# Moving one layer norm's last step, one gating product and one bias add within the order of work of a fused transformer kernel's last stage

## What is computed

```python
y = y_shared + w0 * expert0(x) + w1 * expert1(x)     # two experts' sums
x = x + layernorm(y)
out = (linear_attention(layernorm(x)) @ Wo) * sigmoid(x @ G1 @ G2)   # gated attention output
x = x + (layernorm(out) * gamma + beta, normed once more)
# 4th block: two time steps (a pair of tiles), t = 0, 1
c = f * c + i * g
h = tanh(x @ wo.T + c_final @ uo.T + bo)             # "the state's output" is c_final @ uo.T + bo
x = x + layernorm(h)                                 # a pair's last norm, then its store
```

## Time and profile before

| what | value |
|---|---|
| time, median of 3 runs | 1462.52 us (1462.14 to 1462.62) |
| the profiled execution | 1463.27 us |
| its span, first to last instruction | 1461.4 us |
| granted TensorE clock, mean | 0.988 of full speed |
| busy, whole span: PE / PEld | 1410.7 us (97%) / 1235.5 us (85%) |
| busy, whole span: DVE / ACT / POOL | 871.8 us (60%) / 715.1 us (49%) / 603.8 us (41%) |

### The profile page before, as it was taken

One profiled execution on the slowest core, in us unless ns is written; L12 is line 12 of the kernel. 1 busy time (PEld: TensorE's weight loads), 2 busy tenths in 40 slices (PEclk: granted clock), 3 DMA queues, 4 the chain that ended last, 5 costly groups with the idle time before them and its releaser, 6 DMA issues. The chain is left out here.

```text
span 1461.4 us, 36312 instructions
## 1 busy us (share of the span) xinstructions
PE 1410.7 (97%) x13257; PEld 1235.5 (85%) x13257; DVE 871.8 (60%) x1979; ACT 715.1 (49%) x1656; POOL 603.8 (41%) x1133
## 2 busy tenths in 40 slices
PE   7999999899999999999999999999999999999985
PEld 6888888788999999999999999876777778777875
DVE  5888888365333344334433332466888888888772
ACT  4666666222454444444444543343555555555542
POOL 3655665124221222122112210735667776775442
PEclk9999999899999999999999999999999999999997
DMA  6434334253111111111111111531111221121000
GB/s 188 125 110 125 115 109 121 80 156 118 37 38 44 44 41 41 52 44 41 41 44 49 44 41 51 179 98 44 56 49 49 63 60 52 46 62 38 9 16 22
DMA packets 88733, 100.11 MB, mean 68 GB/s; under 512 B 12432, under 2 KB 75664, under 8 KB 88560
## 3 DMA queue, kind: packets, MB, share of 16 engines
q1 hardware_dynamic: 80704, 78.51, 17.4%
q0 software_dynamic: 6480, 17.70, 4.3%
q10 hardware_dynamic: 1376, 1.57, 0.3%
HBM read 63.28 MB, written 34.47 MB: 67 GB/s over the span
## 5 line engine op out<-in xcount | busy, mean ns | idle before, releaser
L1073 DVE TENSOR_TENSOR ex_gT<-ex_gT,wa_xk 128x256 f32<-128x256 f32 x71 | 29.9, 422 | 306.2 <-ACT ex_gT L1036 306.2
L938 POOL COPY slot_idx<-source 128x1 int32<-128x1 int32 x69 | 37.6, 545 | 403.1 <-PE wa_Z L995 388.2
L968 PE MATMUL wa_P<-ex_xT,lane_w 128*128 128x128 f32 x1704 | 202.0, 275 | 0.0
L968 PEld LDWEIGHTS wa_P<-ex_xT,lane_w 128*128 128x128 f32 x1704 | 196.1, 192 | 0.2 <-issue 0.2
L1004 PE MATMUL wa_Y<-w,ex_gT 128*128 x852 | 195.8, 380 | 0.4 <-issue 0.4
L1004 PEld LDWEIGHTS wa_Y<-w,ex_gT 128*128 128x128 f32 x852 | 156.4, 190 | 18.9 <-issue 0.7
L968 PE MATMUL wa_qv<-ex_xT,lane_w 128*128 128x128 f32 x852 | 118.2, 275 | 0.0
L968 PEld LDWEIGHTS wa_qv<-ex_xT,lane_w 128*128 128x128 f32 x852 | 111.9, 192 | 3.6
L964 ACT COPY lane_w<-w 128x1408 f32 x71 | 96.9, 1365 | 7.8 <-issue 1.6
L1034 ACT ACTIVATE ex_gT<-wa_qv 128x256 f32<-128x256 f32 x71 | 27.2, 383 | 130.2 <-PE wa_qv L968 130.1
L1034 ACT ACTIVATE ex_gT<-wa_P 128x384 f32<-128x384 f32 x71 | 34.8, 490 | 113.6 <-PE wa_P L968 110.5
(11 more groups left out here) (284 smaller groups left out, 3319.0 us busy)
## 6 DMA issues: line engine op xcount, KB each, us to landing
yg<-ex_yo SPq DMA_DIRECT2D x71, 128.0 KB, 1.7
w<-in_w SPq DMA_DIRECT2D x16, 384.0 KB, 4.9
w<-in_w SPq DMA_DIRECT2D x16, 352.0 KB, 3.1
w<-in_w SPq DMA_DIRECT2D x16, 320.0 KB, 4.1
wa_xa<-in_x SPq DMA_DIRECT2D x32, 128.0 KB, 2.1
x<-wa_xo SPq DMA_DIRECT2D x32, 128.0 KB, 1.7
xn<-wa_xn SPq DMA_DIRECT2D x32, 128.0 KB, 2.0
xn1T<-wa_x1T SPq DMA_DIRECT2D x32, 128.0 KB, 2.1
```

The lines of the kernel that those rows point to most:

```text
L938: e.tensor_copy(d["idx"][:], source[:, i:i + 1]).then_inc(S["idx"], 1)
L968: o = e.matmul(out, lane_w[:, i % 2, k, at:at + P], B[i % 2]["xT"][:, k, :], start=(k == 0), stop=(k == KC - 1))
```

## The change

Four things change; no instruction is added or removed.

- A pair's last norm and store (L1599 on VectorE, L1851 on GpSimd, the two stores on SyncE) go from lag 13 to lag 14 in steps before 37: pairs 0 to 11 are done in the even steps 14 to 36. Pairs 12 to 15 stay at lag 13, in the steps 37 to 43.
- The gating product `y` (L1634) goes between the first and the second expert's sum (L1618, L1622).
- The statistics "1" of `y` stay where they were.
- `ucb` (L1668) goes ahead of the statistics "x" and "3"; `hb` (L1673) stays last.

```diff
+        DRAIN = NT + 5
...
+        def norm_pair(s):
+
+            return pair(s, 14 if s < DRAIN else 13)
...
@@ sync
-                for u in pair(s, 13):
+                for u in norm_pair(s):
                     e.wait_ge(S["ho"], u + 1)
...
+        def gated_output(e, i):
+
+            d = B[i % 2]
+            e.wait_ge(S["z"], i + 1)
+            e.wait_ge(S["gt"], i + 1)
+            e.tensor_tensor(d["y"][:], bE[:, 3, 0:C], d["gt"][:], ALU.mult).then_inc(S["y"], 1)
...
@@ vector
-                for u in pair(s, 13):
+                for u in norm_pair(s):
                     p = H[u % 2]
                     e.wait_ge(S["rsh"], 2 * u + 2)
...
                     e.scalar_tensor_tensor(d["ym"][:], YG[0][i % 4][:], weight[:, 0, t:t + 1], d["ys"][:], ALU.mult,
                                            ALU.add).then_inc(S["y0"], 1)
+                for i in tile(s, 5, NT):
+                    gated_output(e, i)
+                for i in tile(s, 1, NT):
+                    d, t = B[i % 2], i // 2 + i % 2 * PAIRS
                     e.wait_ge(S[f"a1{i % 4}"], 16 * (i // 4 + 1))
                     e.wait_ge(S["y0"], i + 1)
                     e.scalar_tensor_tensor(d["ym"][:], YG[1][i % 4][:], weight[:, 1, t:t + 1], d["ym"][:], ALU.mult,
                                            ALU.add).then_inc(S["y1"], 1)
+                for i in tile(s, 1, NT):
                     e.wait_ge(S["y1"], i + 1)
-                    norm_stats(e, S, "0", i, d["ln0"], d["ym"][:], 3)
+                    norm_stats(e, S, "0", i, B[i % 2]["ln0"], B[i % 2]["ym"][:], 3)
...
                 for i in tile(s, 5, NT):
-                    d = B[i % 2]
-                    e.wait_ge(S["z"], i + 1)
-                    e.wait_ge(S["gt"], i + 1)
-                    e.tensor_tensor(d["y"][:], bE[:, 3, 0:C], d["gt"][:], ALU.mult).then_inc(S["y"], 1)
                     e.wait_ge(S["y"], i + 1)
-                    norm_stats(e, S, "1", i, d["ln1"], d["y"][:], 2)
+                    norm_stats(e, S, "1", i, B[i % 2]["ln1"], B[i % 2]["y"][:], 2)
...
+                for u in pair(s, 11):
+                    e.wait_ge(S["uo"], u + 1)
+                    e.tensor_tensor(H[u % 2]["ucb"][:], carry_bank(u), bo[:], ALU.add).then_inc(S["ucb"], 1)
                 for i in tile(s, 2, NT):
                     e.wait_ge(S["x2"], i + 1)
                     norm_stats(e, S, "x", i, B[i % 2]["lnx"], X2[i % 8][:], 3)
...
                 for u in pair(s, 11):
                     p = H[u % 2]
-                    e.wait_ge(S["uo"], u + 1)
-                    e.tensor_tensor(p["ucb"][:], carry_bank(u), bo[:], ALU.add).then_inc(S["ucb"], 1)
                     e.wait_ge(S["ucb"], u + 1)
...
```

More of the change, by code:

```diff
@@ L1294, in sync @@
                 e.wait_ge(S[f"out{L}"], 32 * (PAIRS // 2))
-        DRAIN = NT + 5
         def gate_part(e, t, names, bank, at0, carry):
```

## The result

The changed kernel takes 1469.18 us (median of 5 runs, 1468.32 to 1469.73), the kernel before in the same session 1462.62 (5 runs). The ratio is 1.0043, 95% interval 1.0031 to 1.0054: slower by 6.6 us, 0.4%. The forecast was 1469.3 us.

A forecast was written before the change was run, and what follows sets the result against it. TensorE's own work bounds, with VectorE's loop from z to L1390 close under it. Odd steps -1.0, even steps +3.6 and steps 5 to 12 +4.2 give +6.8 us on 1462.52: 1469.3 us, range 1466 to 1474.

The forecast's parts named there:

- What bounds: Loop of z, gating product, rest of VectorE's list, mask product, L1390: second limit, close under TensorE's own work.
- Part 1: Pair's norm one step later: 0 us, with 0 to +0.3 us a step in even steps as bounds.
- The cover named: Even steps: first sum done by 1295.5, z ends 1295.93, 0.4 us cover if the gating product precedes the second sum.
- The rule weighed: First sum beside GpSimd's add: SBUF contention could add 0.71 us, costing even steps 2 us more; left out.
- Part 2: Gating product between the sums: 6.3 us gained at L1475, but 0.96 us more per step before the mask product.
- Part 3: `ucb` ahead of two statistics, odd steps only: 0.12 us saved, its new wait costing 0.
- The sum: Odd steps -1.0 us, even steps +3.6, steps 5 to 12 +4.2: +6.8 us in total.
- (a): VectorE's stretch does not bind, so TensorE keeps the 6.3 us gain: 1456.2 us; chance 0.17.
- (c): SBUF contention in even steps adds 2 to 3 us to the +6.8: 1471.5 us; chance 0.12.
- (d): Norm's move makes GpSimd's add delay the gather or scale "0", 0.5 us in 12 even steps: 1475; chance 0.03.
- (b): A draw: moved instructions cost near 0.7 us, or early and even steps lose less: 1461.5 to 1465.4; chance 0.16.

The follow-up runs named there:

- the first part alone: Only the pair's last norm, add and store moved to lag 14 before step 37, against the kernel before: 1461.8 us against 1463.59, ratio 0.9986.
- the kernel with the norm in the gap: Pair's norm behind the mask product, GpSimd's add waiting for the second sum, against the kernel before: 1457.48 us, ratio 0.9966; without that wait 1463.64, 1.0003.
- the second part alone: Only the gating product put between the experts' sums, norm and `ucb` at their old places, against the kernel before: 1471.02 us against 1463.59, ratio 1.0041.

## Why the prediction was right

*What bounds.* The loop from z over the gating product, VectorE's list and the mask product to the next L1390 was the right reading: after the mask products of steps 7 to 33 L1395 now starts 0.81 to 0.84 us later, but for step 11's (1.03 us), where there was slack.

*Part 1.* "I take 0 for all of it": true inside the whole change, and only there. The cover named, the gating product ahead of the second sum, was real: alone, the first part costs 0.57 to 0.63 us in each even step. The norm in step 28 takes 0.73 us, not 1.16. (The two instructions of step 27 were not 0.58 us each, as the prediction reads them, but 0.81 and 0.42.) But the first sum beside GpSimd's add takes 1.45, which the sum left out. It ends as late as z: the gating product starts at 1302.95, z ends at 1302.92.

*The rule weighed.* GpSimd's add ends at 1302.53, the first sum 0.30 us after it, at 1302.83, though it began at 1301.38; in the first part alone it ended 0.28 us after the add, and with the add moved away it took 0.48 us. So VectorE's instruction behaved as if it nearly stood still while GpSimd's two adds ran. By the Trainium skill, "SBUF — State Buffer", "Who interferes with whom", a VectorE instruction with two SBUF inputs contends with a GpSimd instruction that reads SBUF, and the trace agrees, with 1.45 against 0.48 us. I had priced it at one add, 0.71 us; it was 0.97. By itself it costs nothing in the changed kernel (1468.86 without it) and about 4 us in the kernel with the norm in the gap, where the same add beside the rotary products costs 2 more. The prediction also says that the trace of before shows no first sum beside the add. It does, in step 31, and there the sum takes 0.92 us:

```profile
1338.71 0.92 DVE L1618 SCALAR_TENSOR_TENSOR la_ym<-la_a,weight,la_ys 128x256 f32<-128x256 f32 x1
```

```profile
1337.94 1.41 POOL L1851 TENSOR_TENSOR la_h<-la_h,la_xo 128x256 f32<-128x256 f32 x2 [0.56 <-DVE la_h L1599]
```

It is the step with the longest wait of L1475 in the earlier trace rows. The price could have been read there ahead of any run.

*Part 2.* The gain of 6.3 us is there: L1480's waits are gone. The price of the three instructions behind the gating product, put at 0.96 us, is 0.95 (1.41 less 0.46).

*Part 3.* 0.12 us were forecast; 5.65 against 5.54 us without and with it in odd steps is 0.11. "No one on TensorE waits for `ucb` before the last gates" held for the changed kernel, but the second part alone shows that the last gates do wait, 2.5 us, when `ucb` stays last. I had not seen that the third part removes such a wait.

*The sum.* Odd steps: z to L1390 7.43 us against 7.52 forecast; the sum let the mask product start at the end of `hb`, and it starts 0.08 us before it (1293.54 against 1292.93 plus 0.69), as the prediction says of instructions that do not need each other. Even: 7.41 against 7.44. From z to L1390 steps 5 to 12 lose 3.8 us against +4.2, and steps 13 to 32 1.9 against +2.6: 5.7 us where the sum has 6.8. Two terms that it lacks make up most of the rest: from L1390 to the next z a step of 13 to 32 is 0.07 us longer on average (27 to 28: 7.52 against 7.45), with the early steps 1.6 us in all, and between steps 8 and 9 the clock gives 1.1 back. That makes 6.2 us in the profile from step 5 to 33, and 6.6 in the medians. So the direction, the mechanism and the large terms are as forecast; that the total came within 0.1 us of the measured time is luck.

*The rivals.* (a), TensorE keeps the gain, is refuted by the second part alone. The condition given for it, that the moved instructions cost less than 0.69 us, was the right one: with 0.41 us behind the gating product the gain appears. (c), contention, exists and cost nothing here. (d), a new wait on GpSimd, did not come: no matmul of the changed kernel's last stage waits for GpSimd. (b), a draw, is what the first part alone comes near.

## What to carry to other kernels

Before moving a reader forward in an engine's order to free a bank sooner, follow the same engine to its next item that the bottleneck waits for: what was ahead of the reader may have run in the time it had to wait anyway, and behind it the same work stands in the way. Measure both distances, reader to release and reader to the next gate, against the bottleneck's own pace; here 0.03 us of slack on the second decided over 0.59 us of gain on the first. And read what runs on GpSimd at the new place of a VectorE instruction with two SBUF inputs.

## What the runs showed of the hardware that was not expected

A VectorE instruction with two SBUF inputs of 256 floats that takes 0.48 us alone took 1.45 when it began 0.25 us after the start of GpSimd's two adds (1.40 us together), and 0.92 when it began 0.77 us after, in the first part alone and in step 31 of the kernel before: it ended 0.28 to 0.30 us after the adds in all three. The adds themselves kept their 1.40 us. Beside the rotary products both sides were slower: in step 30 of the kernel with the norm in the gap the adds took 2.32 us, the product of 512 floats 1.22 instead of 0.68, and the one of 256 floats 0.94 instead of 0.41. That matters by where it lies: 0 us in one order, some 6 us in another, 4 from the sum and 2 from the products.

The granted clock around step 9 went with the order of VectorE's list: 0.89 in the changed kernel, 0.77 in the one before, with 18.9 and 20.0 us from the z of step 8 to the z of step 9, which repeats in four kernels and in six.
